# Value products of full steps cut into two halves of the query columns, one half behind each unit of scores

## The chip, the core and the metric

The kernel runs on one core of one Trainium2 chip. The metric is device time in microseconds (us), the median of a few runs. The engines are named as in the profile: PE is the matrix engine (TensorE), PEld its weight loads, ACT the scalar engine, DVE the vector engine, POOL GpSimd, SP the queue that issues most transfers.

## What is computed

Two batches of 2048 tokens of width 256 pass through four layers. The change lies in the first, a causal attention with 16 heads of width 16 whose queries, keys and values are all the normalised input:

```
x = x + attn_a(layernorm(x))
x = x + ffn(layernorm(x), ...)      # mixture of 2 of 8 experts
x = x + attn_b(layernorm(x), ...)   # attention by distance
x = x + ffn(layernorm(x), ...)

def attn_a(x):                      # B=2, S=2048, H=16, hd=16
    q = k = v = x.reshape(B, S, H, hd).transpose(0, 2, 1, 3)
    w = einsum('bhqd,bhkd->bhqk', q, k) / sqrt(hd)
    w = softmax(where(causal, w, min))
    return einsum('bhqk,bhkd->bhqd', w, v)
```

## The kernel before

**Groups, chunks, steps.** Head attention works through 8 groups G (two batches by four sets of four heads) and, in each, 4 chunks c of 512 query columns. A pair of group and chunk is a job. A job goes through its keys in steps of 128: 4c steps of kind "full" (all 512 query columns), then three steps on the diagonal, "first", "pair" and "last". A group has 36 steps, 24 of them full; head attention has 288. `steps` is this list, numbered n; group 7, the last, is steps 252 to 287, its chunk 2 is steps 262 to 272 and its chunk 3 is steps 273 to 287.

**Units.** A step's scores come in two units (one for "last"). A unit is one pair of PSUM banks of 1024 scores per partition, for two of the four heads. On PE it takes two matmuls of 512 columns on 64 rows each (L912); on ACT it is one exponential of 128x1024 (L775), which writes `a_probs`. Three pairs of banks form a ring (`SR = 3`), so PE waits for exponential u-3 before it writes the scores of unit u. There are 544 units. `a_probs` is a ring of 8 units.

**Value products.** `products(pe, n)` (L543) multiplies the probabilities of a step by the values: four matmuls in 32-bit floats, one for each head, side by side in four column tiles of 32. The profile shows each as two records, so a full step's products are a row with x8. They are issued two steps late (`LAG = 2`), behind both units of scores of step n, and add up in one of two banks, `spare[:, job % 2]`, read at the job's end by DVE (`copy_out`, L632). Three steps into the next job PE transposes that output back (`turn_out`, L883).

**Order.** All of it is written out by hand in PE's queue: in each step two units of scores, now and then a transposition, then the products of step n-2. In the last group `last_group` adds small matmuls at the end of some steps, which prepare the next layers: at step 16 + k of the group (k = 1 to 4) a product of two weight matrices (L1550), and in its steps 26, 27, 28, 30, 32 and 34 others (L1575, L1577, L1171, L1181, L1201). Behind head attention the mixture's first matmuls follow (f_h, L1040 to L1042), with the products of the last two steps between them.

Of the kernel before, what the change touches and what calls it, by code (L numbers as in the profile page):

```python
# [43 lines left out]
CHUNK = 512  # L44
# [11 lines left out]
class Program:  # L56
# [41 lines left out]
    def sb(self, ctx):  # L98
        return lambda name, shape, dt: ctx.enter_context(self.nc.sbuf_tensor(name, shape, dt))
# [9 lines left out]
    def ps(self, ctx):  # L109
        return lambda name, shape, dt: ctx.enter_context(self.nc.psum_tensor(name, shape, dt))  # L110
# [320 lines left out]
def head_attention(pr, block, distance_inputs, cols, weights, mix, moving, fixed):  # L431
# [5 lines left out]
    GH = 4  # L437
    GD = GH * HD
    NG = NB * GROUPS
    with ExitStack() as ctx:  # L440
        sb, ps = pr.sb(ctx), pr.ps(ctx)
        values = sb("a_values", [P, 2, TILES, GH, 32], F32)
# [5 lines left out]
        UR, SR = 8, 3  # L448
        probs = sb("a_probs", [P, UR, 2, CHUNK], F32)
# [5 lines left out]
        spare = ps("a_out", [P, 2, CHUNK], F32)  # L455
# [10 lines left out]
        number = {of: i for i, of in enumerate(outputs)}  # L466
# [8 lines left out]
        steps, output_end = [], []  # L475
# [6 lines left out]
        first_unit = [units.index((n, 0)) for n in range(len(steps))] + [len(units)]  # L482
        masks_by, masks = [], 0
# [8 lines left out]
        SCAN_AT = {9: 0, 10: 1, 11: 2, 13: 3, 14: 4, 15: 5, 17: 6, 21: 7}  # L492
        scales = pr.scales
        LAST = len(outputs) - CHUNKS
        LAG = 2

        TURNED = 4

# [8 lines left out]
        def turned(engine, job):  # L507

            if job < TURNED:
                engine.wait_ge(s_emov, job + 1)  # L510
            else:
                engine.wait_ge(s_turned, 16 * (job - TURNED + 1))
# [17 lines left out]
        def tiles_of(operand, job):  # L530

            G, cc = outputs[job]
            return operand[G % 2][:, TPC * cc:TPC * (cc + 1)]

        def products(pe, n):
            G, c, kind, kt = steps[n]
            i = number[G, c]
            pe.wait_ge(s_exp, first_unit[n + 1])
            pe.wait_ge(s_mask, masks_by[n])
            for tile, skip, w, unit_of, col_of in pieces[kind]:  # L540
                for j in range(GH):
                    u, col = first_unit[n] + unit_of[j // 2], col_of[j // 2]
                    mm = pe.matmul(spare[32 * j:32 * j + 32, i % 2, skip:skip + w], values[:, G % 2, kt + tile, j, :],  # L543
                                   probs[:, u % UR, j % 2, col:col + w], start=(kt == 0 and kind in ("full", "first")),
                                   stop=(kind == "last"), skip_group_check=True)
            mm.then_inc(s_pv, 1)

        @block.sync
        def _(sp):
            def copy_fixed(job):  # L550

                turned(sp, job)
                if job >= BY_ENGINES + 2:
                    sp.wait_ge(s_efix[job % 2], FIXED * ((job - BY_ENGINES) // 2))
                for h in range(2):
                    for to, of, rows in ROTATED:
                        a, b = 4 * HD * h + to, 4 * HD * h + of
                        sp.dma_start(tiles_of(fixed, job)[a:a + rows], tiles_of(moving, job)[b:b + rows]).then_inc(s_efix[job % 2], 16)

            def turn(job):  # L560
                sp.wait_ge(s_lo, job + 1)
                sp.dma_start(tiles_of(moving, job).rearrange("p t r n -> p (t r) n"),
                             split_m[:, job % 2].rearrange("p t h i j e -> p (t h i j e)"), transpose=True).then_inc(s_turned, 16)
# [232 lines left out]
        def _(pe):  # L796
            reads = [[], []]

            def free(bank):
                for s_read, count in reads[bank]:  # L800
                    pe.wait_ge(s_read, count)
                reads[bank].clear()
# [48 lines left out]
            def turn(job):  # L851

                if job == 2:
                    pe.wait_ge(s_exp, 8)
                else:
                    free(job % 2)
                    reads[job % 2].append((s_emov, job + 1))
                pe.wait_ge(s_lo, job + 1)
                for t in range(TPC):
                    for r in range(GH // 2):  # L860
                        mm = pe.transpose(turn_bank(job).bitcast(F16)[:, (r * TPC + t) * P:(r * TPC + t + 1) * P],
                                          split_m[:, job % 2, t, 2 * r:2 * r + 2].rearrange("p a i j e -> p (a i j e)"), pr.ident16[:])
                mm.then_inc(s_tmov, 1)

            def turn_fixed(job):
                pe.wait_ge(s_lo_f, job + 1)
                if job == 1:
                    pe.wait_ge(s_exp, 3)
                for t in range(TPC):
                    for r in range(GH // 2):  # L870
                        mm = pe.transpose(fixed_turned[job].bitcast(F16)[:, (r * TPC + t) * P:(r * TPC + t + 1) * P],
                                          split_f[:, job, t, 2 * r:2 * r + 2].rearrange("p a r e -> p (a r e)"), pr.ident16[:])
                mm.then_inc(s_tfix, 1)
                if job == 0:
                    reads[1].append((s_pfix, 1))

            def turn_out(i):

                free(i % 2)
                reads[i % 2].append((s_added, i + 1))  # L880
                pe.wait_ge(s_ocopy, i + 1)
                for t in range(TPC):
                    mm = pe.transpose(spare[:, i % 2, t * P:(t + 1) * P], osb[:, i % 2, t * P:(t + 1) * P], pr.ident[:])  # L883
                mm.then_inc(s_oturn, 1)
# [6 lines left out]
            for n, (G, c, kind, kt) in enumerate(steps):  # L891
                job = number[G, c]
                if kt == 0 and kind in ("full", "first"):
                    turned(pe, job)
                if kind == "first":
                    if job == 0:
                        pe.wait_ge(s_pfix, 1)
                    elif job == 1:
                        pe.wait_ge(s_pfix, 2)
                    else:  # L900
                        pe.wait_ge(s_efix[job % 2], FIXED * ((job - BY_ENGINES) // 2 + 1))
                for u in range(first_unit[n], first_unit[n + 1]):
                    if u >= SR:
                        pe.wait_ge(s_exp, u - SR + 1)
                    for tile, skip, w, unit_of, col_of in pieces[kind]:
                        q0 = c * TPC + skip // P
                        for a in range(2):
                            if first_unit[n] + unit_of[a] != u:
                                continue
                            for h in range(2):  # L910
                                head = slice(64 * h, 64 * h + 64)
                                mm = pe.matmul(scores[:, 2 * (u % SR) + h, col_of[a]:col_of[a] + w], fixed[G % 2][head, kt + tile, a, :],  # L912
                                               moving[G % 2][head, q0:q0 + w // P, a, :], start=True, stop=True)
                    mm.then_inc(s_scores, 1)
                if n == 0:
                    turn(1)
                if n == 2:
                    turn_fixed(1)
                if n == 5:
                    turn(2)  # L920
                if turned_outputs < len(outputs) and n == output_end[turned_outputs] + LAG + 1:
                    turn_out(turned_outputs)
                    turned_outputs += 1
                if n >= LAG:
                    of, kc, kind, first = steps[n - LAG]
                    if kind in ("full", "first") and first == 0:
                        free(number[of, kc] % 2)
                    products(pe, n - LAG)
                if n == 11:
                    turn(3)  # L930
                if turned_outputs and n == output_end[turned_outputs - 1] + LAG + 2:
                    if turned_outputs - 1 == MEAN_AT:
                        free(1)
                        routing.sums(pe)
                        reads[1].append((routing.s_pooled, routing.times))
                    if turned_outputs - 1 == CHOOSE_AT:
                        free(1)
                        routing.products(pe)
                        reads[1].append((routing.s_logits, routing.times))
                if G == NG - 1:  # L940
                    last_group(n % GS)
            assert turned_outputs == len(outputs) - 1

        def finish(pe, part):

            if part == 0:
                for n in range(len(steps) - LAG, len(steps)):
                    products(pe, n)
# [1231 lines left out]
```

## Time and profile before

| what | value |
| --- | --- |
| median of 3 runs | 1634.15 us (1632.42 to 1634.27) |
| the profiled execution: time, span | 1634.83 us, 1633.1 us |
| head attention: first exponential to end of the last | about 14 to 517 us |
| PE busy, ACT busy over the span | 1573.8 us (96%), 986.0 us (60%) |
| granted clock of PE | 0.999 |

The span runs from the first to the last instruction; 1.7 us of the profiled time lie around it. A row of the timeline gives the start, the length, the engine, the line, the operation, the tiles and the number of instructions merged into it. Records of PE are laid out as pipelined: a matmul's length contains its latency, so the time that a batch costs is read from its start to the start of the next one.

### The profile page before, as it was taken

The numbers are of one execution on the slowest core, as the hardware profiler recorded it, in microseconds if no ns is written. First come the engines' busy times: TensorE is split into PE (matmuls) and PEld (weight loads), VectorE is DVE, ScalarE is ACT, GpSimd is POOL, SyncE is SP. The second block draws the span as 40 slices with busy tenths as digits, with TensorE's granted clock in tenths as the row PEclk, the third lists the DMA queues.
The fourth block names the chain that finished last, engine by engine and source line by source line (L and its number), as shares of the span: only waits on it lengthen the run. The fifth ranks groups of instructions, "written<-read, shape, count | busy, mean of one in ns | idle before, by whom it ended". The sixth has DMA issues, their size and how long they took to land.

```text
span 1633.1 us, 30168 instructions
## 1 busy us (share of the span) xinstructions
PE 1573.8 (96%) x11531; PEld 859.1 (53%) x11531; DVE 1053.6 (65%) x2130; ACT 986.0 (60%) x1260; POOL 358.3 (22%) x467
## 2 busy tenths in 40 slices
PE   6999999999999999999999999999999899999998
PEld 2222222222223666666665666666666566666666
DVE  7532454343335975786556689868999897577544
ACT  6999999999998433443336555555454543353332
POOL 3012122122022000101003644455444400011000
PEclk9999999999999999999999999999999999999999
DMA  4232634211230003111110001100001201411100
GB/s 143 49 117 44 190 95 130 52 28 27 53 105 14 14 14 117 14 20 21 20 20 14 1 2 20 20 14 2 1 1 40 85 12 26 126 27 33 33 14 27
DMA packets 122285, 72.83 MB, mean 45 GB/s; under 512 B 85455, under 2 KB 113182, under 8 KB 122142
## 3 DMA queue, kind: packets, MB, share of 16 engines
q1 hardware_dynamic: 122142, 70.89, 16.7%
q8 instruction: 93, 1.52, 0.4%
q14 instruction: 50, 0.41, 0.1%
HBM read 38.88 MB, written 4.19 MB: 26 GB/s over the span
## 4 chain that ended last, share of the span: by engine, by line
PE 62%; ACT 17%; issue 13%; DVE 6%; POOL 1%; DMA 0%; ACTq 0%; DVEq 0%; SPq 0%; POOLq 0%
ACT a_probs L775 16%; PE f_ypsum L1041 7%; PE f_ypsum L1040 7%; PE f_ypsum L1042 7%; PE f_h L1040 7%; PE f_h L1042 7%; PE f_h L1041 7%; PE d_outs L1040 3%; PE d_outs L1042 3%; PE d_outs L1041 3%; PE d_banks L1040 2%; PE d_banks L1042 2%; PE d_banks L1041 2%; DVE d_dist L2074 1%; PE a_scores L912 1%
## 5 line engine op out<-in xcount | busy, mean ns | idle before, releaser
L775 ACT ACTIVATE a_probs<-a_scores 128x1024 f32<-128x1024 f32 x544 | 499.9, 1282 | 3.0 <-PE a_scores L912 2.9
L1412 ACT ACTIVATE f_gelu<-f_h,f_bcol,s_more 128x512 f32<-128x512 f32 x256 | 198.9, 777 | 407.3 <-PE f_h L1042 392.5
L543 PE MATMUL a_out<-a_probs,a_values 128*32 128x512 f32 (+3 forms) x2560 | 293.2, 539 | 8.7 <-ACT a_probs L775 8.6
L1467 DVE TENSOR_SCALAR f_hh<-f_gelu,f_gates_scaled 128x512 f16<-128x512 f32 x256 | 135.1, 528 | 184.2 <-ACT f_gelu L1412 183.5
L1929 ACT ACTIVATE d_score<-d_dist,d_nksq,s_more 128x512 f32<-128x512 f32 x128 | 104.1, 813 | 187.0 <-DVE d_dist L2074 185.2
L912 PE MATMUL a_scores<-a_moving,a_fixed 64*128 64x512 f16 (+3 forms) x1280 | 191.8, 353 | 19.9 <-ACT a_probs L775 5.4
L1042 PE MATMUL f_ypsum<-f_w,f_hl 128*128 128x256 f16 x768 | 209.3, 273 | 0.0
L1040 PE MATMUL f_ypsum<-f_w,f_hh 128*128 128x256 f16 x768 | 209.3, 273 | 0.0
L1041 PE MATMUL f_ypsum<-f_w,f_hh 128*128 128x256 f16 x768 | 209.3, 273 | 0.0
L1469 DVE SCALAR_TENSOR_TENSOR f_hl<-f_gelu,f_gates_scaled,f_hh 128x512 f16<-128x512 f32 x256 | 193.3, 755 | 9.1
L1966 POOL TENSOR_TENSOR distance_raw<-distance_raw,d_p 128x512 f32<-128x512 f32 x112 | 149.0, 1331 | 176.9 <-ACT d_p L1906 176.8
L912 PEld LDWEIGHTS a_scores<-a_moving,a_fixed 64*128 64x128 f16 x1280 | 49.5, 93 | 259.5 <-ACT a_probs L775 207.3
L792 POOL TENSOR_SCALAR_AFFINE_SELECT a_probs<-a_probs 128x256 f32<-128x256 f32 (+1 forms) x224 | 96.8, 446 | 406.0 <-ACT a_probs L775 397.0
L632 DVE COPY a_osb<-a_out 128x512 f32<-128x512 f32 x32 | 22.1, 691 | 213.3 <-PE a_out L543 213.2
L1486 POOL TENSOR_TENSOR x<-x,f_b_wide 128x256 f32<-128x256 f32 x64 | 53.7, 859 | 434.9 <-DVE c_xn L1006 364.7
L1040 PE MATMUL f_h<-c_xhi,f_w 128*128 128x512 f16 x384 | 145.6, 379 | 2.6 <-DVE f_w L1118 2.5
L1041 PE MATMUL f_h<-c_xlo,f_w 128*128 128x512 f16 x384 | 145.5, 379 | 0.0
L1042 PE MATMUL f_h<-c_xhi,f_w 128*128 128x512 f16 x384 | 145.5, 379 | 0.0
L1040 PE MATMUL d_outs<-d_vhi,d_phi 128*128 128x256 f16 x512 | 140.1, 274 | 0.8 <-DVE d_plo L2021 0.8
L1042 PE MATMUL d_outs<-d_vhi,d_plo 128*128 128x256 f16 x512 | 140.2, 274 | 0.0
L1041 PE MATMUL d_outs<-d_vlo,d_phi 128*128 128x256 f16 x512 | 140.1, 274 | 0.0
L543 PEld LDWEIGHTS a_out<-a_probs,a_values 128*32 128x32 f32 x2560 | 55.8, 108 | 97.1 <-issue 72.7
(259 smaller groups left out, 2633.3 us busy)
## 6 DMA issues: line engine op xcount, KB each, us to landing
f_raw<-in_L_ffn_W SPq DMA_DIRECT2D x16, 1024.0 KB, 8.8
f_raw<-in_L_ffn_W SPq DMA_DIRECT2D x24, 512.0 KB, 8.1
a_fixed<-a_moving SPq DMA_DIRECT2D x60, 96.0 KB, 2.3
x<-in_L_attn_a_x SPq DMA_DIRECT2D x7, 512.0 KB, 5.9
out<-x SPq DMA_DIRECT2D x7, 512.0 KB, 3.1
f_raw<-in_L_ffn_W SPq DMA_DIRECT2D x12, 256.0 KB, 3.4
a_fixed<-a_moving SPq DMA_DIRECT2D x60, 32.0 KB, 2.0
f_early_raw<-in_L_ffn_W SPq DMA_DIRECT2D x4, 256.0 KB, 3.4
```

The lines of the kernel that those rows point to most:

```text
L543: mm = pe.matmul(spare[32 * j:32 * j + 32, i % 2, skip:skip + w], values[:, G % 2, kt + tile, j, :], probs[:, u % UR, j % 2, col:col + w], ...
L775: act.activation(probs[:, u % UR], scores[:, 2 * (u % SR):2 * (u % SR) + 2, :], ACT.Exp, scale=HD ** -0.5)\
L792: pool.affine_select(out=tri, in_=tri, compare_op=ALU.is_ge, fill=0.0, base=0, pattern=[[0, tri.shape[1]], [1, P]], channel_multiplier=-1) ...
L912: mm = pe.matmul(scores[:, 2 * (u % SR) + h, col_of[a]:col_of[a] + w], fixed[G % 2][head, kt + tile, a, :], moving[G % 2][head, q0:q0 + w ...
L1040: pe.matmul(out, fixed_hi, moving_hi, start=first, stop=False, skip_group_check=shared)
L1041: pe.matmul(out, fixed_hi, moving_lo, start=False, stop=False, skip_group_check=shared)
L1042: return pe.matmul(out, fixed_lo, moving_hi, start=False, stop=last, skip_group_check=shared)
L1412: act.activation(gel[:, n % HR, :], hps[:, n % 2, :], ACT.Gelu, bias=mix.bcol[:, q, FT * e + j:FT * e + j + 1], scale=pr.scales.hidden)\
L1467: dve.tensor_scalar(hh[:, n % HR, :], gel[:, n % HR, :], gate, None, ALU.mult).then_inc(s_hh, 1)
L1469: dve.scalar_tensor_tensor(out=hl[:, n % HR, :], in0=gel[:, n % HR, :], scalar=gate, in1=hh[:, n % HR, :], op0=ALU.mult, op1=ALU.subtract) ...
L1929: act.activation(score[:, n % 2, :], dist[:, n % DR, :], ACT.Exp, scale=pr.scales.distance, bias=nksq[:, b, kt:kt + 1]).then_inc(s_score, 1)
L1966: pool.tensor_tensor(acc, acc, p32[:, n % R, :], ALU.add).then_inc(s_acc, 1)
```

## The change

From step 40 on, where both step n and step n-2 are full, the four value products of 512 query columns become two batches of four products of 256 query columns. The first batch is issued behind the first unit of scores of step n, the second behind its second unit, where the whole batch stood. That holds for chunk steps 2 to 4c-1, which is 2, 6 and 10 steps for c = 1, 2 and 3, and 18 in a group; in groups 1 to 7 it is 126 steps. Each half loads the four values tiles into PE again, waits on the same two semaphores (`s_exp`, `s_mask`), and the second half signals `s_pv`. Where a job's first products are halved, the wait for the bank (`free`) stands ahead of the first half. All other steps are as they were.

```diff
-        LAG = 2
+        LAG, HALVES_FROM = 2, 40
...
+        def in_halves(n):
+
+            return n >= HALVES_FROM and steps[n][2] == "full" and steps[n - LAG][2] == "full"
+
+        def half_products(pe, n, half):
+            G, c, kind, kt = steps[n]
+            i, cut = number[G, c], slice(half * CHUNK // 2, (half + 1) * CHUNK // 2)
+            pe.wait_ge(s_exp, first_unit[n + 1])
+            pe.wait_ge(s_mask, masks_by[n])
+            for j in range(GH):
+                u = first_unit[n] + j // 2
+                mm = pe.matmul(spare[32 * j:32 * j + 32, i % 2, cut], values[:, G % 2, kt, j, :], probs[:, u % UR, j % 2, cut],
+                               start=(kt == 0), stop=False, skip_group_check=True)
+            if half == 1:
+                mm.then_inc(s_pv, 1)
...
                     mm.then_inc(s_scores, 1)
+                    if in_halves(n) and u == first_unit[n]:
+                        of, kc, _, first = steps[n - LAG]
+                        if first == 0:
+                            free(number[of, kc] % 2)
+                        half_products(pe, n - LAG, 0)
...
-                if n >= LAG:
+                if in_halves(n):
+                    half_products(pe, n - LAG, 1)
+                elif n >= LAG:
                     of, kc, kind, first = steps[n - LAG]
```

On PE, in the last group, the end of its chunk 2 reads as follows before: a full step (two units of scores, four products of 512 columns), then another that ends with the first L1550.

```order
L912 MATMUL a_scores<-a_moving,a_fixed 128x512 [waits a_exp]
L912 MATMUL a_scores<-a_moving,a_fixed 128x512
L912 MATMUL a_scores<-a_moving,a_fixed 128x512 [waits a_exp]
L912 MATMUL a_scores<-a_moving,a_fixed 128x512
L543 MATMUL a_out<-a_probs,a_values 32x512 [waits a_mask,a_exp]
L543 MATMUL a_out<-a_probs,a_values 32x512 x3
L1550 MATMUL a_out<-distance_raw,wv_turned 128x256 [waits dw_vcol]
```

At the same place of the changed kernel the same step reads so (L928, L546 and L1573 are now the lines of scores, halved products and L1550):

```order
L928 MATMUL a_scores<-a_moving,a_fixed 128x512 [waits a_exp]
L928 MATMUL a_scores<-a_moving,a_fixed 128x512
L546 MATMUL a_out<-a_probs,a_values 32x256 [waits a_mask,a_exp]
L546 MATMUL a_out<-a_probs,a_values 32x256 x3
L928 MATMUL a_scores<-a_moving,a_fixed 128x512 [waits a_exp]
L928 MATMUL a_scores<-a_moving,a_fixed 128x512
L546 MATMUL a_out<-a_probs,a_values 32x256 [waits a_mask,a_exp]
L546 MATMUL a_out<-a_probs,a_values 32x256 x3
L1573 MATMUL a_out<-distance_raw,wv_turned 128x256 [waits dw_vcol]
```

One batch of products has moved ahead of the second unit of scores, and the step has two batches where it had one.

The other place is step 276, the fourth of the last group's chunk 3, on PE, where the output of the job before is transposed. Before:

```order
L912 MATMUL a_scores<-a_moving,a_fixed 128x512 [waits a_exp]
L912 MATMUL a_scores<-a_moving,a_fixed 128x512
L912 MATMUL a_scores<-a_moving,a_fixed 128x512 [waits a_exp]
L912 MATMUL a_scores<-a_moving,a_fixed 128x512
L883 MATMUL a_out<-ident,a_osb 128x128 [waits a_ocopy]
L883 MATMUL a_out<-ident,a_osb 128x128 x3
L543 MATMUL a_out<-a_probs,a_values 32x512 [waits a_mask,a_exp]
L543 MATMUL a_out<-a_probs,a_values 32x512 x3
```

In the changed kernel:

```order
L928 MATMUL a_scores<-a_moving,a_fixed 128x512 [waits a_exp]
L928 MATMUL a_scores<-a_moving,a_fixed 128x512
L546 MATMUL a_out<-a_probs,a_values 32x256 [waits a_mask,a_exp]
L546 MATMUL a_out<-a_probs,a_values 32x256 x3
L928 MATMUL a_scores<-a_moving,a_fixed 128x512 [waits a_exp]
L928 MATMUL a_scores<-a_moving,a_fixed 128x512
L899 MATMUL a_out<-ident,a_osb 128x128 [waits a_ocopy]
L899 MATMUL a_out<-ident,a_osb 128x128 x3
L546 MATMUL a_out<-a_probs,a_values 32x256 [waits a_mask,a_exp]
L546 MATMUL a_out<-a_probs,a_values 32x256 x3
```

The transposition (now L899) still stands ahead of the last products of its step, but only half of them are left behind it.

## Rows read from the trace of the kernel before

**Rows 1.** The page: engines; groups of instructions (busy, mean ns, idle before, releaser).

```profile
PE 1573.8 (96%) x11531; PEld 859.1 (53%) x11531; DVE 1053.6 (65%) x2130; ACT 986.0 (60%) x1260; POOL 358.3 (22%) x467
...
L775 ACT ACTIVATE a_probs<-a_scores 128x1024 f32<-128x1024 f32 x544 | 499.9, 1282 | 3.0 <-PE a_scores L912 2.9
...
L543 PE MATMUL a_out<-a_probs,a_values 128*32 128x512 f32 (+3 forms) x2560 | 293.2, 539 | 8.7 <-ACT a_probs L775 8.6
```

**Rows 2.** Windows: PE, PEld, DVE, ACT, POOL busy (x); clock, DMA share, GB/s.

```profile
90.00:450.00 360.00, 337.67 (x2856) 85.98 (x2852) 142.30 (x319) 360.00 (x394) 66.19 (x156) 1.00 0.31 83
...
470.00:492.00 22.00, 21.93 (x187) 6.51 (x179) 8.43 (x25) 20.83 (x24) 2.99 (x7) 1.00 0.34 120
```

**Rows 3.** Timeline of ACT: start, length, instruction, count, idle before and releaser.

```profile
109.41 271.77 ACT L775 ACTIVATE a_probs<-a_scores 128x1024 f32<-128x1024 f32 x296
...
489.84 1.94 ACT L775 ACTIVATE a_probs<-a_scores 128x1024 f32<-128x1024 f32 x2 [0.92 <-PE a_scores L912]
...
504.94 1.02 ACT L775 ACTIVATE a_probs<-a_scores 128x1024 f32<-128x1024 f32 x1 [0.22 <-PE a_scores L912]
```

**Rows 4.** Timeline of PE at 103 us: a full step without a wait.

```profile
103.26 0.61 PE L912 MATMUL a_scores<-a_moving,a_fixed 64*128 64x512 f16 x4
103.80 1.06 PE L543 MATMUL a_out<-a_probs,a_values 128*32 128x512 f32 x8
104.80 0.91 PE L912 MATMUL a_scores<-a_moving,a_fixed 64*128 64x512 f16 x4
```

**Rows 5.** Timeline at 303 us: products of 256 columns, a lone unit.

```profile
303.03 0.64 PE L543 MATMUL a_out<-a_probs,a_values 128*32 128x256 f32 x8
...
303.60 0.39 PE L912 MATMUL a_scores<-a_moving,a_fixed 64*128 64x512 f16 x2
...
304.23 0.39 PE L912 MATMUL a_scores<-a_moving,a_fixed 64*128 64x512 f16 x2 [0.24 <-ACT a_probs L775]
...
304.55 1.06 PE L543 MATMUL a_out<-a_probs,a_values 128*32 128x512 f32 x8
```

**Rows 6.** Timeline of PE in chunk 2 of the last group.

```profile
473.38 0.85 PE L912 MATMUL a_scores<-a_moving,a_fixed 64*128 64x512 f16 x4
...
485.29 0.61 PE L912 MATMUL a_scores<-a_moving,a_fixed 64*128 64x384 f16 x8
```

**Rows 7.** Timeline of PE in chunk 3 of the last group.

```profile
489.41 0.60 PE L912 MATMUL a_scores<-a_moving,a_fixed 64*128 64x512 f16 x4
...
492.05 0.39 PE L912 MATMUL a_scores<-a_moving,a_fixed 64*128 64x512 f16 x2
492.75 0.39 PE L912 MATMUL a_scores<-a_moving,a_fixed 64*128 64x512 f16 x2 [0.30 <-ACT a_probs L775]
...
494.06 0.91 PE L912 MATMUL a_scores<-a_moving,a_fixed 64*128 64x512 f16 x4
494.90 0.66 PE L883 MATMUL a_out<-ident,a_osb 128*128 128x128 f32 x4
495.49 1.06 PE L543 MATMUL a_out<-a_probs,a_values 128*32 128x512 f32 x8
496.48 0.61 PE L912 MATMUL a_scores<-a_moving,a_fixed 64*128 64x512 f16 x4
...
504.51 0.61 PE L912 MATMUL a_scores<-a_moving,a_fixed 64*128 64x512 f16 x4
```

**Rows 8.** Timeline of PE at the end of head attention.

```profile
511.17 0.74 PE L912 MATMUL a_scores<-a_moving,a_fixed 64*128 64x512 f16 x4
...
512.84 0.91 PE L912 MATMUL a_scores<-a_moving,a_fixed 64*128 64x384 f16 x8
...
516.62 0.39 PE L1040 MATMUL f_h<-c_xhi,f_early 128*128 128x512 f16 x1
...
518.02 1.50 PE L543 MATMUL a_out<-a_probs,a_values 128*32 128x384 f32 x24
```

**Rows 9.** The chain that ended last, behind head attention: start, length, what.

```profile
520.92 0.45 PE a_out L952 x4
521.40 0.27 DVE a_rden L639
521.69 0.44 DVE a_onorm L641
```

## The prediction

> **What bounds the kernel now.** I read the page first. PE is busy 96% of the span, but head attention is another case: its 544 exponentials fill 499.9 us of ACT and ACT idled 3.0 us before them [rows 1]. The windows say the same: from 90 to 450 us ACT is busy for all 360.00 us, PE for 337.67, at clock 1.00 [rows 2]. The timeline gives ACT's pace: 296 exponentials in one unbroken row of 271.77 us. Taking off one length of 1.28, (271.77 - 1.28) / 295 = 0.917 us each [rows 1, 3]. A full step has two, so ACT needs 1.834 us a step. PE, when it doesn't wait, needs 1.54: 103.26 to 103.80 for the scores, 1.00 more for the products [rows 4]. So in groups 1 to 6 ACT is the bound and PE waits for it. There the reader should look at PE's start times, not at ACT's idle time: exponentials overlap, and an idle of 0 alone would not prove that none came late. That 295 in a row keep one pace does.
>
> The last group is different. Its extra matmuls make PE the slower one: from 470 to 492 us PE is busy 21.93 of 22.00 and ACT only 20.83 [rows 2], and ACT idles 0.92 us at 489.84 and 0.22 at 504.94 for scores [rows 3]. The exponential behind the scores of 504.51 ended at 504.94 + 1.02 = 505.96, so scores lead to the end of their exponential in 1.45 us [rows 3, 7].
>
> **What a halved step costs on PE.** All prices have a row. A lone unit of scores followed by products costs 0.32 (304.23 to 304.55); two units together cost 0.54 (103.26 to 103.80), so the second adds 0.22 and 0.10 is fixed. Products of 256 columns followed by scores cost 0.57 (303.03 to 303.60); those of 512 cost 1.00, so 256 columns are 0.43 and 0.14 is fixed [rows 4, 5]. The "last" steps' products at 303.03 have exactly the shape of a half: four heads, x8, 256 columns. A halved step is 2 x (0.32 + 0.57) = 1.78 us against 1.54: **+0.24 us of PE**, the two fixed parts once more. The repeated weight loads are inside the 0.57. No other queue gets an instruction; the extra waits name semaphores that the unit just ahead already waited for (exponential u-3 of the first unit is the last of step n-2), and are free.
>
> These fixed parts sit where PE changes between two row tiles (scores) and four column tiles (products). The Trainium skill (TensorEngine Tiling, Key Properties) says that changing the tiling mode drains TensorE. By that rule the halves pay two drains more, as the rows do; without it the two halves would cost what the whole did and the sum below would be zero or a gain. The trace agrees with the rule, at 0.10 and 0.14 us.
>
> **Groups 1 to 6.** 1.78 is under 1.834, so ACT stays the bound. A group's PE work grows by 18 x 0.24 = 4.3 us, from about 55 (32 two-unit steps and their products at 1.54, four "last" ones at 0.32 + 0.57, four transpositions at 0.59, which is 494.90 to 495.49 [rows 7]) to about 60; ACT needs 68 x 0.917 = 62.4. The order helps locally: a unit of scores can start when exponential u-3 is done and is late only 3 x 0.917 - 1.45 = 1.3 us after that. Behind a whole batch it started 0.32 + 1.00 - 0.92 = 0.40 late; behind a half 0.89 is less than 0.917, so it starts on time. That is a reserve which was not short before. Nothing is gained and nothing lost: 0. What hides the extra of the 110 halved steps outside the last group's chunks 2 and 3 (126 less 16) is ACT's own pace; without that cover they would cost 110 x 0.24 = 26 us.
>
> **The last group.** Here nothing hides it. Chunk 2 has six halved steps, 264 to 269: +1.44. PE waited once there before, in 473.38's row, 0.85 long where 0.61 is usual: 0.24 [rows 6]. After it PE is never free until 492, so all later work, and the exponentials from 489.4 on, move by 1.44 - 0.24 = **1.20**. Chunk 3, in steps:
> - Step 275. First unit at 492.05 + 1.20 = 493.25, half behind it, second unit at 494.14 (its exponential allows 492.75 + 1.20 = 493.95). Only half the products follow, so step 276 starts at 494.14 + 0.89 = 495.03: +0.97 on 494.06.
> - Step 276. Second unit at 495.92; then 0.32, the transposition 0.59 and a half 0.57: step 277 at 497.40, **+0.92** on 496.48 [rows 7].
> - Steps 277 to 284: 8 x 0.24 = +1.92, so +2.84 at step 285.
> - Before, PE waited for exponentials at 511.17 (0.74 long for 0.61) and 512.84 (0.91 for the 0.61 of 485.29's row): 0.13 + 0.30 = 0.43 [rows 6, 8]. PE is late now and will not wait: 2.84 - 0.43 = **+2.4** at the last scores.
> Taking the fixed parts to the next digit makes it 2.2 rather than 2.4 (each halved step 0.235 or so); I take **+2.3 us**.
>
> **Behind it.** The mixture's first matmuls follow at 516.62 with the last products at 518.02 [rows 8], and the chain goes on over the last transposition (L952) to DVE [rows 9]. Nothing there waits for anything but PE, so all of it moves by 2.3. Against the profiled execution this is 1634.83 + 2.3 = 1637.1; that execution stood 0.7 above the median of the runs, and the median is what is asked: 1634.15 + 2.3 = **1636.4**, +0.14%. A measurement of this kernel can tell about 0.2%, 3.3 us, from no change, so my forecast is "no change that can be told", on the slow side.
>
> **Rivals.**
> - *The halves cost more, and PE becomes the bound in all groups (slower).* For it: a PE that runs 1.78 of 1.834 has only 3% left, and two sets of semaphore waits per step could add sequencer time that no row of before shows with such a density. Against: the "last" step's row has the same neighbours and waits. The point from which it decides is 1.834 a step plus the reserve of about 0.25 us that the boundaries of chunks leave. At 1.88 a step only the last group pays: 2.3 + 16 x 0.10 = +3.9. At 1.93 each chunk 3 overruns by 10 x 0.10 - 0.25 = 0.7, six times 4, and the last group 2.3 + 16 x 0.15 = 4.7: +8.8, 1643.
> - *The fixed parts are not paid again (a gain).* Then PE has no more work, and the earlier first units let it fill its waits in the last group: 0.24, then 0.48 at 492.05 (the second unit 0.70 behind the first for 0.22) and 0.30 at 494.06, 0.43 at the end: -1.4 us, 1632.7. For it: the half can start while scores still drain. Against: both rows of a lone unit and of a short batch [rows 5].
> - *The loss is absorbed behind head attention.* PE is not all of the mixture's start; if DVE's or a transfer's work decides there, the time stays at 1634.2. Against: the chain of rows 9 hangs on PE's products.
>
> **How the numbers follow.** Forecast (+0.6 to +3.3 around 2.3) 0.60; more costly halves 0.22; absorbed 0.11; gain 0.07. The forecast's own range is 1634.8 to 1637.5. Slower by over 0.2% is the costly case and the upper edge of the forecast, 0.22 + 0.05 = 0.27. Faster by over 0.2% needs more than the gain that I can name: 0.02. Within 0.2%: 0.71. The range of 8 in 10, 1634.0 to 1639.2, takes the forecast, the absorbed case and the costly case up to about 1.90 a step.
>
> **What would show it.** In the profile after: exponentials of groups 1 to 6 still at 0.917 each in one unbroken row (else the costly case); a half's products followed by scores at 0.57 and a unit followed by a half at 0.32; PE's share from 90 to 450 us up from 337.67; scores of the last group at 489.4 now near 490.6 and the first f_h at 516.62 now near 518.9; ACT's idle for scores larger by about 2. What would prove me wrong: the first f_h at or before 516.6, or exponentials slower than 0.92 before 450 us.

## The result

| | us |
| --- | --- |
| before, median of 19 runs | 1633.07 (1632.42 to 1635.39) |
| changed, median of 19 runs | 1636.55 (1634.76 to 1637.04) |
| ratio of the times | 1.0017, 95% interval 1.0011 to 1.0023 |
| forecast | 1636.4, range 1634.0 to 1639.2 |

The ratio is +2.8 us (1.8 to 3.8) on 1633.07: slower than before beyond the interval, and within the 0.2% that the prediction called no change. The two medians lie further apart, 3.5 us, because executions of one kernel fall on two levels (last section) and the medians happen to lie on different ones.

The page of the changed kernel, its engines and the groups that answer to [rows 1] (L791 is the exponential, L546 the halved products, L559 the whole ones):

```profile
PE 1589.7 (97%) x12539; PEld 880.5 (54%) x12539; DVE 1054.2 (64%) x2130; ACT 986.4 (60%) x1260; POOL 358.2 (22%) x467
...
L791 ACT ACTIVATE a_probs<-a_scores 128x1024 f32<-128x1024 f32 x544 | 500.3, 1298 | 4.8 <-PE a_scores L928 4.7
...
L559 PE MATMUL a_out<-a_probs,a_values 128*32 128x512 f32 (+3 forms) x1552 | 158.9, 496 | 8.6 <-ACT a_probs L791 8.4
...
L546 PE MATMUL a_out<-a_probs,a_values 128*32 128x256 f32 x2016 | 161.0, 391 | 0.0
```

PE is busy 15.9 us longer (1589.7 - 1573.8) and the time grew by 2.8. ACT's idle time for scores went from 2.9 to 4.7.

Windows of the changed kernel, columns as in [rows 2], first groups 1 to 6, then the last group:

```profile
90.00:450.00 360.00, 350.16 (x3704) 103.90 (x3696) 142.25 (x318) 360.00 (x394) 66.29 (x156) 1.00 0.32 83
470.00:492.00 22.00, 22.00 (x214) 7.12 (x210) 7.88 (x22) 19.82 (x22) 2.98 (x7) 1.00 0.30 105
```

PE took 12.5 us more between 90 and 450 us, where ACT still is busy throughout. By PE's start times it should be about twice that: 360 us hold some 104 halved steps, and 104 x 0.24 is 25 us (an estimate). The busy figure shows less because before it counted part of PE's waiting, as in the row of 0.91 for 0.61 [rows 4]. In the last group PE is full and ACT lost another 1.0 us.

Timelines of ACT in the changed kernel, which answer to [rows 3]. The first is the view of 110 to 380 us, the second that of 15 to 520 us:

```profile
108.67 272.75 ACT L791 ACTIVATE a_probs<-a_scores 128x1024 f32<-128x1024 f32 x297
```

```profile
26.45 435.65 ACT L791 ACTIVATE a_probs<-a_scores 128x1024 f32<-128x1024 f32 x475 [0.19 <-PE a_scores L928]
...
479.92 3.77 ACT L791 ACTIVATE a_probs<-a_scores 128x1024 f32<-128x1024 f32 x4 [0.38 <-PE a_scores L928]
484.11 1.94 ACT L791 ACTIVATE a_probs<-a_scores 128x1024 f32<-128x1024 f32 x2 [0.42 <-PE a_scores L928]
...
503.80 1.94 ACT L791 ACTIVATE a_probs<-a_scores 128x1024 f32<-128x1024 f32 x2 [0.47 <-PE a_scores L928]
506.20 12.32 ACT L791 ACTIVATE a_probs<-a_scores 128x1024 f32<-128x1024 f32 x13 [0.47 <-PE a_scores L928]
```

The first row is the pace of groups 1 to 6: (272.75 - 1.30) / 296 = 0.917 us, unchanged. The second view has one unbroken row of 475 exponentials from 26.45 to 462.10 us, so all new idle times are in the last group.

Timeline of PE in the changed kernel: a halved step of group 1, and two places of the last group, which answer to [rows 4, 5, 7, 8]:

```profile
102.61 0.39 PE L928 MATMUL a_scores<-a_moving,a_fixed 64*128 64x512 f16 x2
102.92 0.64 PE L546 MATMUL a_out<-a_probs,a_values 128*32 128x256 f32 x8
103.50 0.39 PE L928 MATMUL a_scores<-a_moving,a_fixed 64*128 64x512 f16 x2
...
489.96 0.61 PE L928 MATMUL a_scores<-a_moving,a_fixed 64*128 64x512 f16 x4
...
513.37 0.60 PE L928 MATMUL a_scores<-a_moving,a_fixed 64*128 64x512 f16 x4
...
517.07 0.39 PE L928 MATMUL a_scores<-a_moving,a_fixed 64*128 64x256 f16 x4
...
518.39 0.39 PE L1063 MATMUL f_h<-c_xhi,f_early 128*128 128x512 f16 x1
```

A unit and its half take 103.50 - 102.61 = 0.89, twice that is 1.78.

**How head attention is compared below.** Executions start their work at different offsets (the first exponential at 14.4 us before, 13.8 in the changed one). So I take the length from the first exponential to the mixture's first f_ypsum matmul, both from the list of a tile's instructions, which has one digit: 524.8 - 14.4 = 510.4 us before, 526.6 - 13.8 = 512.8 in the changed kernel, **+2.4 us**. The two rows of the changed kernel:

```profile
L791 ACT ACTIVATE a_probs<-a_scores x544: 1014/1302/1563, 13.8 to 517.5; 128x1024 f32<-128x1024 f32 x182
...
L1063 PE MATMUL f_ypsum<-f_early,f_hh x128: 272/273/273, 526.6 to 830.4; 128*128 128x256 f16 x128
```

In this length are also the first dozen exponentials, up to 27 us, where no kernel below differs from before. They took 12.69 us before (14.43 to 27.12 in ACT's timeline) and in most kernels, but 0.1 us more in e4_whole_first, 0.2 in e9_spread and 0.3 in e2_last and e5_three. That much of the lengths of these four is not of their edits.

### The profile page after: what moved, and what is told of

Same layout as the page of the kernel before. It is cut to its first block, busy times and chain, and to the rows that moved or that the text cites. A ratio compares the mean times of both kernels' runs of the same rounds, so it can differ in the third digit from the quotient of the medians.

```text
span 1634.9 us, 32310 instructions
## 1 busy us (share of the span) xinstructions
PE 1589.7 (97%) x12539; PEld 880.5 (54%) x12539; DVE 1054.2 (64%) x2130; ACT 986.4 (60%) x1260; POOL 358.2 (22%) x467
## 4 chain that ended last, share of the span: by engine, by line
PE 67%; ACT 14%; issue 12%; DVE 6%; POOL 1%; DMA 0%; DVEq 0%; ACTq 0%; POOLq 0%
ACT a_probs L791 13%; PE f_ypsum L1064 7%; PE f_ypsum L1065 7%; PE f_ypsum L1063 7%; PE f_h L1063 7%; PE f_h L1064 7%; PE f_h L1065 7%; PE d_outs L1063 3%; PE d_outs L1065 3%; PE d_outs L1064 3%; PE a_scores L928 3%; PE d_banks L1063 2%; PE d_banks L1065 2%; PE d_banks L1064 2%; PE a_out L559 2%
## 5 line engine op out<-in xcount | busy, mean ns | idle before, releaser
L791 ACT ACTIVATE a_probs<-a_scores 128x1024 f32<-128x1024 f32 x544 | 500.3, 1298 | 4.8 <-PE a_scores L928 4.7
L928 PE MATMUL a_scores<-a_moving,a_fixed 64*128 64x512 f16 (+3 forms) x1280 | 198.6, 354 | 6.7 <-ACT a_probs L791 1.5
L928 PEld LDWEIGHTS a_scores<-a_moving,a_fixed 64*128 64x128 f16 x1280 | 51.7, 93 | 220.3 <-ACT a_probs L791 121.8
L559 PE MATMUL a_out<-a_probs,a_values 128*32 128x512 f32 (+3 forms) x1552 | 158.9, 496 | 8.6 <-ACT a_probs L791 8.4
L546 PE MATMUL a_out<-a_probs,a_values 128*32 128x256 f32 x2016 | 161.0, 391 | 0.0
```

The source lines that it names most:

```text
L546: mm = pe.matmul(spare[32 * j:32 * j + 32, i % 2, cut], values[:, G % 2, kt, j, :], probs[:, u % UR, j % 2, cut], start=(kt == 0), stop=Fa ...
L791: act.activation(probs[:, u % UR], scores[:, 2 * (u % SR):2 * (u % SR) + 2, :], ACT.Exp, scale=HD ** -0.5)\
```

## The experiments

My theory: a halved step pays the two fixed costs between scores and products (0.10 and 0.14 us) once more; ACT's pace hides that wherever PE has nothing else, and the last group's extra matmuls take that cover away. Rivals: the loss is spread over all groups; short batches or the new order cost by themselves; the extra matmuls only mark waits on DVE.

Each kernel of the experiments ran 11 times, but e5_three and e6_four only twice. With 11 runs the intervals reach about 0.09% (1.5 us) to either side, so effects of 1 to 2 us are read from the traces, one profiled execution each.

| kernel | length of head attention | against 510.4 | ratio to before (95%) |
| --- | --- | --- | --- |
| changed | 512.8 | +2.4 | 1.0017 (1.0011 to 1.0023) |
| e1_early | 510.4 | 0.0 | 0.9998 (0.9989 to 1.0007) |
| e2_last | 513.1 | +2.7 | 1.0014 (1.0005 to 1.0023) |
| e3_together | 510.4 | 0.0 | 1.0001 (0.9992 to 1.0010) |
| e4_whole_first | 510.7 | +0.3 | 1.0001 (0.9992 to 1.0010) |
| e5_three | 529.4 | +19.0 | 1.0116 (1.0098 to 1.0135) |
| e6_four | 555.8 | +45.4 | 1.0285 (1.0267 to 1.0304) |
| e7_fewer_before | 509.0 | -1.4 | 0.9992 (0.9983 to 1.0001) |
| e8_fewer_after | 510.4 | 0.0 | 0.9999 (0.9990 to 1.0008) |
| e9_spread | 508.8 | -1.6 | 0.9994 (0.9985 to 1.0003) |
| e10_spread_halves | 511.3 | +0.9 | 1.0007 (0.9998 to 1.0016) |

### Which groups pay

```diff
-            return n >= HALVES_FROM and steps[n][2] == "full" and steps[n - LAG][2] == "full"
+            return HALVES_FROM <= n < GS * (NG - 1) and steps[n][2] == "full" and steps[n - LAG][2] == "full"
```

> The halves only in groups 1 to 6 (110 of the 126 halved steps less the last group's two of chunk 1, so 108), the last group as before. My theory (two fixed costs of 0.10 and 0.14 us more per halved step, hidden by ACT's 1.834 us a step wherever no other matmuls stand): 0.0 us, exponentials from 90 to 450 us in one row at 0.917 each, PE busier by about 12 us there. Rival (the 2.8 us are spread over all groups, 0.02 us a step): +2.4 us, and exponentials at more than 0.917 each.

For the last group alone:

```diff
-        LAG, HALVES_FROM = 2, 40
+        LAG, HALVES_FROM = 2, 252
```

> The halves only in the last group (18 steps). My theory: the whole loss of the change, +2.2 us (the step-by-step sum to one more digit), first f_h 2.2 us later against the first exponential. Rival (spread over all groups): +0.4 us.

108 halved steps in groups 1 to 6 cost 0.0 us, 18 in the last group the whole. (Of the two numbers in the first text, 110 is less the last group's chunks 2 and 3 alone; its chunk 1 has two more, which leaves 108.) The windows of e1_early show PE as busy as in the changed kernel there, and its ACT runs in one row, (271.84 - 1.30) / 295 = 0.917:

```profile
90.00:450.00 360.00, 350.12 (x3704) 104.03 (x3704) 142.20 (x318) 360.00 (x394) 66.49 (x156) 1.00 0.33 83
...
109.44 271.84 ACT L791 ACTIVATE a_probs<-a_scores 128x1024 f32<-128x1024 f32 x296
```

The spread-out loss is out. Of e2_last's 2.7 us, 0.3 is from the first steps (26.77 - 13.76 = 13.01 us for 12.69), so the last group's halves cost 2.4.

### Cut or order

e3_together keeps every instruction of the change and puts both halves behind the second unit:

```diff
-                    if in_halves(n) and u == first_unit[n]:
...
-                        half_products(pe, n - LAG, 0)
...
                 if in_halves(n):
...
+                    half_products(pe, n - LAG, 0)
                     half_products(pe, n - LAG, 1)
```

> The same 126 steps in halves, but both halves behind the second unit of scores, so that no change between scores and products is added; weight loads, matmuls and semaphore waits are as many as in the change. My theory (the price is that of the changes between scores and products): +0.2 us, a pair of halves followed by scores at about 1.01 instead of 1.14. Rival (a short batch costs 0.14 by itself): the 0.14 per step stays, 16 x 0.14 = +2.2 less the waits it fills, about +1.3 us.

e4_whole_first keeps the place and drops the cut:

```diff
-                        half_products(pe, n - LAG, 0)
+                        products(pe, n - LAG)
...
                 if in_halves(n):
-                    half_products(pe, n - LAG, 1)
+                    pass
```

> The whole products, not cut, behind the first unit of scores in the same 126 steps: the change's order without its cut. The number of changes between scores and products is that of before, since a step's second unit and the next step's first stand together. My theory: 0.0 to +0.1 us. Rival (the place ahead of the second unit costs or gains by itself): the second unit starts 0.4 us later than it may in every step, and if that were short of the reserve of 1.24 us exponentials would come late: above +1 us.

Timeline of PE in e3_together, scores and a pair of halves:

```profile
101.69 1.07 PE L546 MATMUL a_out<-a_probs,a_values 128*32 128x256 f32 x16
102.69 0.61 PE L928 MATMUL a_scores<-a_moving,a_fixed 64*128 64x512 f16 x4
103.23 1.07 PE L546 MATMUL a_out<-a_probs,a_values 128*32 128x256 f32 x16
104.23 0.90 PE L928 MATMUL a_scores<-a_moving,a_fixed 64*128 64x512 f16 x4
```

Two halves one behind the other take 1.00 us, to 0.01 what the whole took [rows 4]. Doubled matmuls, weight loads and waits cost nothing, and neither the cut nor the order costs by itself (0.0 us, and 0.3 of which 0.1 is from the first steps). Only both together add a change between scores and products, and only they cost: the two fixed parts read from [rows 4, 5] belong to that change.

What in the change costs is less clear, since scores and products differ in tile shape, data type and PSUM banks at once. The trace of the changed kernel settles a part. In the last group one half is followed by scores (16-bit floats) and the next by a transposition of weights (L1564) in 32-bit floats, as the products are:

```profile
477.44 0.64 PE L546 MATMUL a_out<-a_probs,a_values 128*32 128x256 f32 x8
478.01 0.39 PE L928 MATMUL a_scores<-a_moving,a_fixed 64*128 64x512 f16 x2
478.33 0.64 PE L546 MATMUL a_out<-a_probs,a_values 128*32 128x256 f32 x8
478.90 0.66 PE L1564 MATMUL a_out<-ident,distance_raw 128*128 128x128 f32 x4
```

Both start 0.57 us after the half's start, so the 0.14 behind products is paid without a change of data type too. Tile shape and bank are not separated, and neither is the 0.10 behind scores.

### The dose

In groups 1 to 6 the scores of one unit (e5) or of both (e6) are cut as well, with products of 128 columns behind each piece. The core of the edit; `TWICE` is 1 or 2:

```diff
+                    if in_halves(n) and i < TWICE:
+                        for part in range(2):
+                            q0, cut = c * TPC + 2 * part, slice(2 * part * P, 2 * (part + 1) * P)
...
+                            if part == 0:
+                                part_products(pe, n - LAG, 2 * i, 2 * i + 1, False)
+                        mm.then_inc(s_scores, 1)
+                        part_products(pe, n - LAG, 2 * i + 1, 2 * i + 2, i == 1)
```

> Dose, in groups 1 to 6 alone: the first unit of scores of a halved step is cut in two halves of 256 columns as well, each followed by value products of 128 columns; the second unit stays whole, followed by a half. Three changes to products a step instead of two. A step of PE is then 1.54 + 2 x 0.24 = 2.0 us, above ACT's 1.834. My theory: PE becomes the bound in runs of halved steps; step by step this gives +15 us. Rival (the fixed costs overlap when batches get short): under +3 us.

> The same in groups 1 to 6 with both units of scores cut: four changes a step, 1.54 + 3 x 0.24 = 2.25 us of PE against 1.834. My theory: +40 us, step by step. Rival (fixed costs overlap): well under that, +10 us or less.

Timeline of PE in e5_three, one step and the start of the next:

```profile
101.77 0.28 PE L928 MATMUL a_scores<-a_moving,a_fixed 64*128 64x256 f16 x2
101.98 0.43 PE L546 MATMUL a_out<-a_probs,a_values 128*32 128x128 f32 x8
102.34 0.28 PE L928 MATMUL a_scores<-a_moving,a_fixed 64*128 64x256 f16 x2
102.55 0.43 PE L546 MATMUL a_out<-a_probs,a_values 128*32 128x128 f32 x8
102.91 0.39 PE L944 MATMUL a_scores<-a_moving,a_fixed 64*128 64x512 f16 x2
103.23 0.64 PE L546 MATMUL a_out<-a_probs,a_values 128*32 128x256 f32 x8
103.80 0.28 PE L928 MATMUL a_scores<-a_moving,a_fixed 64*128 64x256 f16 x2
```

One, two, three and four changes to products a step give PE 1.54, 1.78, 2.03 (103.80 - 101.77) and, in e6_four's timeline (a step's four parts, 102.38 to 104.67), 2.29 us; head attention becomes 0, 0, 19 and 45 us longer by them in groups 1 to 6. So the steps cost 0.24, 0.25 and 0.26 each, and the time starts to pay only past ACT's 1.834. I had said +15 and +40, with steps of 2.0 and 2.25. The measured 2.03 and 2.29 would make 108 x 0.03 = 3.2 and 108 x 0.04 = 4.3 us of the 4.0 and 5.4 missing, if the step-by-step sums had exactly these steps; 0.3 of the 4.0 is from e5_three's first steps. What the rest of the miss is, no run shows.

### What takes the cover away in the last group

Left out: the first of two matmuls for each half of the weights' product (L1550), and the two of the bias (L1575).

```diff
     def product(self, pe, bank, r, k):
+        if k == 0:
+            return
...
-        if k < KD:
-            pe.matmul(bank[:, 0:D], self.bv_wide[:, k, :], self.raw["o"][:, k, :], start=(k == 0), stop=False)
-        else:
+        if k == KD:
```

> The kernel before, with four of the last group's extra matmuls left out: the first of the two that add up to each half of the product of the weight matrices (group steps 17 and 19) and the two of the bias (26 and 27), 0.63 us each; the output is that of another bias and product. My theory: PE's excess in the last group shrinks, and with it the late exponentials of before: -1.4 us. Rival (these stalls are waits on DVE that the extra matmuls only mark): 0.

> The changed kernel with the same four matmuls left out. My theory: with 2.5 us of PE's work gone the halves are partly covered; against the kernel before -0.4 us, so the halves cost 1.0 us here where they cost 2.2 with all the extra matmuls. Rival (the halves cost the same wherever they stand in the last group): 2.2 us more than the run without them, +0.8 us against the kernel before.

With four matmuls fewer the halves cost 510.4 - 509.0 = 1.4 us instead of 2.4. I had said 1.0. They cost less as the load beside them falls; that they would cost the same anywhere in the group (2.2) is out, by the traces. Without halves the four matmuls are worth 1.4 us, as expected: that speaks for PE's load, and against waits on DVE, as what makes exponentials late before.

### A version without the late exponentials

All work is done; `earlier_group(G, at)` holds the moved calls, DVE reads their results in jobs 19, 23 and 27.

```diff
+            def earlier_group(G, at):
+                bank = spare[:, 0, :]
+                if (G, at) in ((4, 26), (4, 28), (5, 28), (6, 26)):
+                    free(0)
+                if (G, at) == (4, 26):
+                    weights.turn_biases(pe, bank)
...
+                elif G == 4 and at in (28, 30, 31):
+                    weights.bias(pe, bank, (28, 30, 31).index(at))
...
+                elif (G, at) == (5, 28):
+                    weights.turn_values(pe, bank)
...
+                elif G == 6 and at in (26, 28, 30, 32):
+                    weights.product(pe, bank, *divmod((at - 26) // 2, KD))
```

> The kernel before, with nine of the last group's extra steps of work moved to earlier groups, where PE has 0.3 us to spare in each full step: the transposed biases and the three matmuls of the bias to group 4 (steps 26, 28, 30, 31), the transposition of the value weights to group 5 (step 28), the four matmuls of the product to group 6 (steps 26, 28, 30, 32). All the work is done. My theory: PE no longer exceeds ACT in the last group, the late exponentials of before go, step by step -1.8 us, first f_h 1.8 us earlier against the first exponential. Rival (the moved matmuls only shift the stalls to where they now stand): 0 or slower.

> The same move under the changed kernel. My theory: in chunk 3 of groups 4 to 6 a halved step has only 0.06 us to spare, so the moved matmuls exceed it there and the halves cost 2.3 us again: +0.5 us against the kernel before. Rival (the halves are harmless once the last group is relieved): -1.8 us as without them.

ACT's timeline in the last group of e9_spread, then that of e10_spread_halves, in groups 4, 6 and the last:

```profile
462.14 52.47 ACT L779 ACTIVATE a_probs<-a_scores 128x1024 f32<-128x1024 f32 x57
```

```profile
319.55 1.94 ACT L795 ACTIVATE a_probs<-a_scores 128x1024 f32<-128x1024 f32 x2 [0.42 <-PE a_scores L931]
321.96 119.33 ACT L795 ACTIVATE a_probs<-a_scores 128x1024 f32<-128x1024 f32 x130 [0.47 <-PE a_scores L931]
441.72 3.77 ACT L795 ACTIVATE a_probs<-a_scores 128x1024 f32<-128x1024 f32 x4 [0.42 <-PE a_scores L931]
445.91 3.77 ACT L795 ACTIVATE a_probs<-a_scores 128x1024 f32<-128x1024 f32 x4 [0.42 <-PE a_scores L931]
450.10 14.77 ACT L795 ACTIVATE a_probs<-a_scores 128x1024 f32<-128x1024 f32 x16 [0.42 <-PE a_scores L931]
...
464.76 52.40 ACT L795 ACTIVATE a_probs<-a_scores 128x1024 f32<-128x1024 f32 x57
```

In e9_spread the last 57 exponentials run in one row, (52.47 - 1.29) / 56 = 0.914 each: the idle 0.92 and 0.22 us of [rows 3] are gone, and head attention is 1.6 us shorter, 1.8 without the slower first steps. In time that is 0.9994, and the interval holds 1: the trace shows the gain, the plain comparison of times doesn't confirm it (the last section compares level by level). With halves the moved matmuls make exponentials late where they now stand: those of the bias in group 4 (at 319.55 and 321.96 us), those of the product in group 6 (442 to 450 us). Counted at a steady 0.917 an exponential, the ends come 0.5 us later with each of the five, about 1.1 us in group 4 and 1.6 in group 6. The halves cost 511.3 - 508.8 = 2.5 us again (2.7 without the first steps), and none of it in the last group, whose 57 exponentials stand in one row here too. The loss follows PE's load, not the place in the program.

## Why the prediction was right

- **The bound of groups 1 to 6.** ACT at 0.917 us an exponential and PE under it: right; 108 halved steps cost 0.0 (e1_early).
- **+0.24 us a halved step, two fixed costs.** Right: 1.54 to 1.78. That it is the change between scores and products was read from two rows and is now shown, by leaving out the change (e3, e4) and by adding it (e5, e6). The extra waits and weight loads are free, as said (e3).
- **The last group, +2.3.** Measured +2.4 between the two marks. The first scores of step 273 came at 489.96 for 489.41 [rows 7]; the first exponential started at 13.76 for 14.43 in ACT's timelines, so against it they are 0.55 + 0.67 = 1.2 later, as the sum said for chunk 2. Chunk 3 follows the sum step by step: step 285 was to be 2.84 later than at 511.17, and it came at 513.37, which is 2.20 + 0.67 = 2.87 later [rows 8]. The last scores, at 517.07, stand 1.32 ahead of the first f_h as before, and that is 518.39 - 516.62 + 0.67 = 2.4 later [rows 8].
- **Behind head attention everything moves along.** Right: f_ypsum is 2.4 later too, and nothing behind it gave any of it back.
- **The level.** That 1636.4 met 1636.55 to 0.15 us is luck. The sum started from 1634.15, the median of three runs, two of them on the upper level; the median of 19 is 1633.07, so the start was 1.1 us too high. The medians of 19 then lie 3.5 us apart, 1.2 more than the 2.3 of the sum, because the changed kernel's lies on the upper level. The two errors cancelled. What the reasoning earns is +2.3 for the +2.4 of the trace and the +2.5 within each level (last section).
- **The rivals.** Costly halves: each cost what the "last" steps' rows said. A gain from earlier first units: none; PE's waits were filled by its own fixed costs. Absorbed behind the stage: not at all.

## What to carry to other kernels

Count changes between kinds of matmul on the matrix engine, not only matmuls: here each round trip from 64-row scores to 32-column products and back cost 0.24 to 0.26 us, whatever the batch's size (512, 256 or 128 columns). Finer interleaving pays them again, and it is free only while another engine sets the pace; look for the stretch where that cover is thinnest, since the price falls due there: 16 x 0.24 = 3.8 us in the last group, less the waits that it fills. When one engine's busy time is a row of overlapping instructions, take its pace over hundreds of them before believing that it never waited.

## What the runs showed of the hardware

Executions of one kernel fall on two levels, about 1.6 us apart: before 1632.4 to 1633.2 eleven times and 1634.1 and more eight times, changed up to 1635.9 seven times and 1636.0 and more twelve times. The medians of the lower level are 1632.61 and 1635.07, those of the upper 1634.16 and 1636.63: the change costs 2.5 us on either. The profiled executions show a stretch in which the levels part, in the distance attention far behind the change. Windows of the changed kernel and of e2_last at the same place:

```profile
885.00:925.00 40.00, 38.64 (x256) 25.79 (x255) 25.00 (x41) 20.71 (x34) 25.06 (x26) 0.96 0.04 8
```

```profile
885.00:925.00 40.00, 38.65 (x264) 25.83 (x263) 26.33 (x42) 22.37 (x37) 26.01 (x27) 1.00 0.04 8
```

The granted clock is 0.96 in one and 1.00 in the other. Of the twelve profiled executions, six have 0.96 in this window and are on the upper level, and five have 1.00 and are on the lower. In e6_four the same work comes 45 us later, and the clock from 930 to 970 us is 0.96; its two runs, 0.3 us apart, don't show two levels. The changed kernel's timeline of PE there:

```profile
898.82 1.02 PE L1836 MATMUL d_misc<-ones,distance_raw 128*128 128x1 f32 x8 [1.36 <-POOL distance_raw L1973]
...
901.07 0.42 PE L1063 MATMUL d_outs<-d_vhi,d_phi 128*128 128x256 f16 x1
901.29 0.42 PE L1064 MATMUL d_outs<-d_vlo,d_phi 128*128 128x256 f16 x1
```

Matmuls of 256 columns start 0.21 us apart (901.07 to 901.29), which is the level of 1.2 GHz; before the wait they start 0.11 apart, which is 2.4 GHz. PE had waited 1.36 us for POOL just before. In e2_last, with the same wait, the clock stayed. 0.04 x 40 = 1.6 us is lost (an estimate), the distance of the two levels. The Trainium skill (TensorE: Matmul & The Clock Gate, "The HAM clock gate") has two clock levels and a check that does not restart with the kernel, so the same idle time may or may not trip it. The traces agree in that the same gap did and did not; what decides between the two is not shown.

Twelve of 19 against eight of 19 on the upper level would be 4/19 x 1.6 = 0.3 us of the difference in the mean, the size of what the ratio's 2.8 leaves over the 2.5 within a level; whether the change moved these odds or chance did, 19 runs can't tell. It also blurred e9_spread. Sorted afterwards by the granted clock of each run, nine of its 11 runs are on the upper level (0.998 or 0.999, median 1632.69) and two on the lower (1.000, median 1630.70); of the 21 runs of the kernel before that were taken with them, eleven are on the upper (median 1634.19) and ten on the lower (1632.77). Level by level the moved matmuls gain 1.5 and 2.1 us, which agrees with the trace's 1.6 to 1.8. The listed clock sorts most runs, not all: one of before, 1633.10, has 0.999.
